# Dense attentions with four score banks, three single key banks, one-bank exponentials and a weighted sum in two halves

## The chip, the cores and the metric

The kernel runs on one core of a Trainium2 chip. The metric is the device time of one execution in microseconds (us); lower is better. A core has a matrix engine (TensorE, PE in the profile, with its weight loads as PEld), VectorE (DVE), ScalarE (ACT), GpSimd (POOL) and a queue engine that issues DMAs (SP). They share the PSUM memory: eight banks of 128 partitions by 512 fp32 values, into which TensorE writes and from which VectorE and ScalarE read.

## The reference, cut to what matters

The program is a stack of twelve sublayers on an activation of 4 sequences by 512 tokens by 128 channels. Only two are touched by the change, the dense attentions with 16 heads of 8 channels each: `mqa` (one shared key and value head, causal) and `rope` (full, not causal).

```python
# mqa                                              # rope
latent = x @ Wc_down                               q, k, v = proj(Wq, bq), proj(Wk, bk), proj(Wv, bv)
q = (latent @ Wq_up).reshape(B, T, 16, 8)          q = _apply_rope(q, cos, sin) * scale
k, v = split(latent @ Wkv_up)                      k = _apply_rope(k, cos, sin)
att = einsum('bthd,bsd->bhts', q, k) * scale       attn = einsum('bhsd,bhtd->bhst', q, k)
att = where(tril, att, -inf)
att = softmax(att, axis=-1)                        attn = softmax(attn, axis=-1)
y = einsum('bhts,bsd->bthd', att, v)               out = einsum('bhst,bhtd->bhsd', attn, v)
x = x + y @ Wc_proj                                x = x + out @ Wo + bo
```

Each stands between feed-forward sublayers (mixture of experts, channel mixing); after them come a gated layer, a forget-gated attention, a deep six-layer block and others, none of which changes.

## The kernel before, in words

All programs are written out by hand, one instruction order for each engine, with counting semaphores between them (`wait_ge`, `then_inc`). The channels of 16 heads are held "wide": a head takes 32 partitions, so that four heads fill the 128 partitions. Four such sets of heads in four sequences make 16 blocks; a block has four tiles of 128 tokens. That gives 64 **groups** for an attention, and the loop over them in `dense_attend_pe` (L571) has 72 **slots**: slot i does three things for three different groups.

- *Scores* of group i (`dense_scores_pe`, L516, matmul L524): four matmuls, head j = 0 to 3 in its own 32 rows of the array, queries of the tile against the keys. VectorE then takes the largest score of every query (`dense_max_dve`, L721: L732 in `rope`, the fused L729 with the causal mask in `mqa`) and so frees the bank.
- *Keys* of group i-6 (`dense_keys_pe`, L536, matmul L550): the same products turned round, keys of a tile on the partitions and the queries along the free dimension, in head order 2, 3, 0, 1. ScalarE takes the exponential into SBUF (`dense_exp_act`, L648, L654).
- The *weighted sum* or *mix* of group i-8 (`dense_mix_pe`, L554, matmul L567): four matmuls, one for each head, in four column groups of the array, all into bank 7; they use all 128 rows. After the fourth tile ScalarE copies the bank away (`dense_y_act`, L657, L659), and the next block's first mix waits for that.

In every fourth slot there is also a *turn* (`dense_max_pe`, L527, L532): four 128x128 matmuls that turn the largest values of a block, which VectorE then adds to the queries (`dense_lay_max_dve`, L734, L737). A turn takes a bank of the same ring as the scores.

In `mqa` the widths follow the causal mask: in the slots i%4 = 0, 1, 2, 3 the scores are 128, 256, 384, 512 wide, the keys 384, 512, 128, 256, and the mix 128, 256, 384, 512; GpSimd zeroes the later keys after the exponentials (`dense_pool`, L781). In `rope` everything is 512 wide.

The PSUM banks before: 0 to 2 are the ring of scores and turns (use v waits until use v-3 is freed), 3 to 6 are two pairs for the keys (pair m waits until the exponential of pair m-2 is done), 7 holds the mix. TensorE executes its queue in order, so whatever stands behind a waiting matmul waits too. The order of a slot before is: score 0, keys of heads 2 and 3, score 1; mix; turn; score 2, keys of heads 0 and 1, score 3.

The probabilities go to one of three buffers (`probs_of`), so an exponential of group g waits for the mix of group g-3.

Of the kernel before, what the change touches and what calls it, by code (L numbers as in the profile page):

```python
# [16 lines left out]
ACT = mybir.ActivationFunctionType  # L17
AX = mybir.AxisListType

P = 128  # L20
NB, T = 4, 512
TILES = T // P
# [23 lines left out]
def program(nc, d, out, sublayers):  # L46
    with ExitStack() as ctx:
# [6 lines left out]
        def bank(i):  # L54
            return psum[:, i * 512:(i + 1) * 512]
# [275 lines left out]
        def moe_dve(dve, u, n, k, b):  # L331
# [32 lines left out]
            for t in range(TILES):  # L364
# [5 lines left out]
                if t >= 2:  # L370
# [18 lines left out]
        dense_counts = {"mqa": da._make([NB, NB, 0, 0, 0, 0, 0, NB, NB, 5 * NB, 5 * NB, 1, 64 * NB, 68 * NB, 4 * NB, 32 * NB,  # L389
                                         32 * NB, 16 * NB, 16 * NB, 4 * NB, NB, NB, NB, NB, NB]),  # L390
                        "rope": da._make([0, 0, NB, NB, 2 * NB, 2 * NB, 6 * NB, 4 * NB, 4 * NB, 8 * NB, 8 * NB, 1, 64 * NB, 68 * NB,
                                          4 * NB, 32 * NB, 32 * NB, 0, 16 * NB, 4 * NB, NB, NB, NB, NB, NB])}
# [23 lines left out]
        SCORE_BANKS = 3  # L416
# [119 lines left out]
        def dense_keys_pe(pe, causal, group, half, N):  # L536

            b, s, kt = group // GROUPS, group // TILES % SETS, key_tile(causal, group)
            q0 = kt * P if causal else 0
            kk = keys_of(causal, b, s)  # L540
            m = 2 * group + half
            if group % TILES == 0 and half == 0:
                pe.wait_ge(da.banks_free, N.banks_free + bank_use[group + TILES, "turn"] + 1)
            if m >= 2:
                pe.wait_ge(da.probs_ready, N.probs_ready + m - 1)
            apart(pe)
            for at in range(2):
                j = KEY_ORDER[2 * half + at]
                r32, to = slice(32 * j, 32 * j + 32), bank(3 + 2 * (m % 2) + at)
                last = nc.tensor.matmul(to[:, q0:T], kk[r32, kt * P:(kt + 1) * P], da_Q[r32, b * SETS + s, q0:T],  # L550
                                        start=True, stop=True)
            last.then_inc(da.keys_ready, 1)

        def dense_mix_pe(pe, causal, group, N):  # L554
            b, s, kt = group // GROUPS, group // TILES % SETS, key_tile(causal, group)
            q0 = kt * P if causal else 0
            first, last_ = group % TILES == 0, group % TILES == TILES - 1
            if causal:
                pe.wait_ge(da.later_zeroed, N.later_zeroed + group + 1)
            pe.wait_ge(da.probs_ready, N.probs_ready + 2 * group + 2)  # L560
            if first and group >= TILES:
                pe.wait_ge(da.y_kept, N.y_kept + group // TILES)
            apart(pe)
            for at in range(SETS):
                j = KEY_ORDER[at]
                c0 = 0 if causal else s * P + 32 * j
                last = nc.tensor.matmul(bank(7)[32 * j:32 * j + 32, q0:T], da_V[:, b * TILES + kt, c0:c0 + 32],  # L567
                                        probs_of(group)[:, at, q0:T], start=first, stop=last_, skip_group_check=True)
            last.then_inc(da.pv_done, 1)

        def dense_attend_pe(pe, causal, N):  # L571
            made = 5 * NB if causal else 8 * NB
            pe.wait_ge(da.wide_kept, N.wide_kept + made)
            pe.wait_ge(da.v_kept, N.v_kept + (NB if causal else NB * TILES))
            for i in range(SLOTS):
                for half in range(2):
                    if half == 1:
                        if i >= MIX_LAG:
                            dense_mix_pe(pe, causal, i - MIX_LAG, N)
                        if turn_of(i) is not None:  # L580
                            dense_max_pe(pe, i, N)
                    if i < GROUPS * NB:
                        dense_scores_pe(pe, causal, i, 2 * half, N)
                    if 0 <= i - LAG < GROUPS * NB:
                        dense_keys_pe(pe, causal, i - LAG, half, N)
                    if i < GROUPS * NB:
                        dense_scores_pe(pe, causal, i, 2 * half + 1, N)

# [59 lines left out]
        def dense_exp_act(act, causal, group, half, N):  # L648
            q0 = key_tile(causal, group) * P if causal else 0
            m = 2 * group + half  # L650
            if half == 0 and group >= 3:
                act.wait_ge(da.pv_done, N.pv_done + group - 2)
            act.wait_ge(da.keys_ready, N.keys_ready + m + 1)
            nc.scalar.activation(probs_of(group)[:, 2 * half:2 * half + 2, q0:T], banks(3 + 2 * (m % 2), 2)[:, :, q0:T],  # L654
                                 ACT.Exp).then_inc(da.probs_ready, 1)
# [5 lines left out]
        def dense_act(act, n, causal, N):  # L661
            dense_prepare_act(act, n, causal, N)
            for group in range(GROUPS * NB + MIX_LAG - LAG):
                mixed = group - (MIX_LAG - LAG)
                if group < GROUPS * NB:
                    dense_exp_act(act, causal, group, 0, N)
                if mixed >= 0 and mixed % TILES == TILES - 1:
                    dense_y_act(act, mixed // TILES, N)
                if group < GROUPS * NB:
                    dense_exp_act(act, causal, group, 1, N)  # L670
# [101 lines left out]
        def dense_pool(pool, u, n, causal, N):  # L772
# [3 lines left out]
            if causal:  # L776
                for group in range(GROUPS * NB):
                    q0 = key_tile(causal, group) * P
                    block = probs_of(group)[:, :, q0:q0 + P]
                    pool.wait_ge(da.probs_ready, N.probs_ready + 2 * group + 2)  # L780
# [1028 lines left out]
```

## Time and profile before

| | before |
|---|---|
| median of 3 runs | 5142.44 us |
| lowest and highest run | 5136.1 and 5149.91 us |
| span of the profiled execution | 5148.7 us |
| busy in the span: PE, DVE, ACT, POOL | 4508.2, 3456.9, 2317.0, 3075.1 us |
| loop of `mqa` (first score to the end of the last mix) | 212.95 to 443.73 us |
| loop of `rope` | about 762 to 1053.00 us |

The profile is of one execution; its span is from the first to the last instruction and lies 6.3 us above the median of the runs. No time around the span is recorded for it. A busy PE is not PE at its peak: matmuls of different rows overlap, and their ends are modelled. One fp32 matmul leaves two records. Where the text says that a matmul takes so long, it is the distance between the starts of two things that can't overlap.

### The profile page before, as it was taken

The numbers are of one execution on the slowest core, as the hardware profiler recorded it, in microseconds if no ns is written. First come the engines' busy times: TensorE is split into PE (matmuls) and PEld (weight loads), VectorE is DVE, ScalarE is ACT, GpSimd is POOL, SyncE is SP. The second block draws the span as 40 slices with busy tenths as digits, with TensorE's granted clock in tenths as the row PEclk, the third lists the DMA queues.
The fourth block names the chain that finished last, engine by engine and source line by source line (L and its number), as shares of the span: only waits on it lengthen the run. The fifth ranks groups of instructions, "written<-read, shape, count | busy, mean of one in ns | idle before, by whom it ended". The sixth has DMA issues, their size and how long they took to land.

```text
span 5148.7 us, 147111 instructions
## 1 busy us (share of the span) xinstructions
PE 4508.2 (88%) x66028; PEld 2555.2 (50%) x66028; DVE 3456.9 (67%) x4153; ACT 2317.0 (45%) x2523; POOL 3075.1 (60%) x1713
## 2 busy tenths in 40 slices
PE   6898689977468999999999999568999999999998
PEld 3444333333135555555555555235555555555554
DVE  4365536632437778778777776447877787888885
ACT  1242134433134555555555555234555555555553
POOL 0010000000019889888889997049988899998984
PEclk7699679976569999999999999669999999999999
DMA  2000000000001112111111111101111111112111
GB/s 71 1 1 1 0 0 1 1 0 0 0 22 32 30 29 55 29 51 32 52 29 53 31 29 33 44 9 29 33 51 30 35 49 30 54 29 55 30 32 29
DMA packets 78094, 144.43 MB, mean 28 GB/s; under 512 B 18728, under 2 KB 24944, under 8 KB 75824
## 3 DMA queue, kind: packets, MB, share of 16 engines
q1 hardware_dynamic: 77488, 135.23, 10.1%
q8 instruction: 517, 8.47, 0.7%
q14 instruction: 89, 0.73, 0.0%
HBM read 39.75 MB, written 1.05 MB: 8 GB/s over the span
## 4 chain that ended last, share of the span: by engine, by line
PE 47%; issue 23%; POOL 21%; DVE 7%; ACT 1%; DMA 0%; SPq 0%; DVEq 0%; POOLq 0%
POOL arena L1446 8%; PE psum L1033 8%; POOL arena L1439 6%; POOL arena L1452 5%; PE psum L1050 4%; PE psum L1064 4%; PE psum L1102 4%; PE psum L1083 4%; PE psum L1002 3%; PE psum L1148 3%; PE psum L1097 2%; PE psum L1142 2%; PE psum L524 2%; POOL rstd L1457 2%; PE psum L1016 2%
## 5 line engine op out<-in xcount | busy, mean ns | idle before, releaser
L1446 POOL TENSOR_TENSOR arena<-arena,minus_half 128x16 f32<-128x16 f32 x384 | 1131.9, 2948 | 32.0
L1439 POOL TENSOR_TENSOR arena<-arena 128x1024 f32<-128x1024 f32 x384 | 909.8, 2369 | 13.5 <-DVE arena L1324 13.5
L1452 POOL TENSOR_TENSOR arena<-arena 128x1024 f32<-128x1024 f32 x384 | 733.7, 1911 | 42.6
L1320 DVE TENSOR_TENSOR arena<-psum,arena 128x1024 f32<-128x1024 f32 x384 | 468.1, 1219 | 404.1 <-ACT arena L1202 404.1
L1462 POOL MEMSET arena<- 128x33 f32 x4 | 0.4, 128 | 995.3 <-DVE std L1686 995.3
L1208 ACT ACTIVATE arena<-psum 128x1024 f32<-128x1024 f32 x384 | 392.2, 1021 | 298.8 <-PE psum L1050 298.4
L1202 ACT ACTIVATE arena<-psum 128x1024 f32<-128x1024 f32 x384 | 392.3, 1022 | 246.5 <-PE psum L1033 243.4
L1324 DVE TENSOR_TENSOR arena<-psum,arena 128x1024 f32<-128x1024 f32 x384 | 466.8, 1215 | 54.1 <-PE psum L1050 54.1
L1050 PEld LDWEIGHTS psum<-w_ident,arena 128*128 128x128 f32 x3072 | 355.3, 141 | 281.9 <-issue 148.5
L1331 DVE TENSOR_REDUCE arena<-arena 128x16 f32<-128x1024 f32 x384 | 464.8, 1211 | 2.8
L1235 ACT ACTIVATE arena<-psum 128x1024 f32<-128x1024 f32 x192 | 196.7, 1024 | 580.7 <-PE psum L1064 580.7
L1050 PE MATMUL psum<-w_ident,arena 128*128 128x128 f32 x3072 | 407.0, 276 | 48.9 <-POOL arena L1452 48.3
L1083 PE MATMUL psum<-arena 64*64 64x32 f32 x24576 | 408.8, 220 | 33.7 <-issue 33.6
L1033 PE MATMUL psum<-deep_wqkv,arena 128*128 128x512 f32 x768 | 388.8, 630 | 36.3 <-DVE arena L1324 28.4
L1083 PEld LDWEIGHTS psum<-arena 64*64 64x64 f32 x24576 | 383.3, 135 | 71.3 <-issue 71.3
L1033 PE MATMUL psum<-arena 128*128 128x512 f32 x768 | 372.8, 607 | 0.0
L1002 PE MATMUL psum<-arena 64*32 64x64 f32 x24576 | 296.4, 224 | 65.8 <-issue 65.2
L524 PE MATMUL psum<-arena 32*128 32x512 f32 (+3 forms) x1024 | 330.2, 593 | 11.9 <-DVE arena L729 9.0
L1002 PEld LDWEIGHTS psum<-arena 64*32 64x32 f32 x24576 | 281.9, 105 | 86.7 <-issue 76.4
L1308 DVE TENSOR_TENSOR arena<-arena 128x1024 f32<-128x1024 f32 x192 | 301.9, 1572 | 5.9
L1219 ACT ACTIVATE arena<-psum 128x1024 f32<-128x1024 f32 x192 | 195.8, 1020 | 242.0 <-PE psum L1016 235.8
L1444 POOL TENSOR_SCALAR arena<-arena 128x16 f32<-128x16 f32 x384 | 153.6, 400 | 245.5 <-DVE arena L1331 245.3
(260 smaller groups left out, 7703.9 us busy)
## 6 DMA issues: line engine op xcount, KB each, us to landing
arena<-arena SPq DMA_DIRECT2D x672, 128.0 KB, 2.3
deep_wqkv<-in_deep_wqkv SPq DMA_DIRECT2D x6, 1536.0 KB, 7.1
arena<-in_deep_wqkv SPq DMA_DIRECT2D x6, 1536.0 KB, 7.2
arena<-arena SPq DMA_DIRECT2D x96, 64.0 KB, 2.5
deep_wo<-in_deep_wo SPq DMA_DIRECT2D x6, 512.0 KB, 7.5
arena<-in_deep_wo SPq DMA_DIRECT2D x6, 512.0 KB, 7.4
deep_w<-in_deep_w SPq DMA_DIRECT2D x6, 341.0 KB, 7.6
arena<-in_deep_w SPq DMA_DIRECT2D x6, 341.0 KB, 7.5
```

The lines of the kernel that those rows point to most:

```text
L524: nc.tensor.matmul(bank(v % SCORE_BANKS)[:, 0:keys], da_Q[r32, b * SETS + s, x_ * P:(x_ + 1) * P], keys_of(causal, b, s)[r32, 0:keys], sta ...
L1002: last = nc.tensor.matmul(bank(r)[32 * jj:32 * jj + 32, pair * 64:pair * 64 + 64], qT[r64, pair, wi * WIN:(wi + 1) * WIN], kT[r64, pair, w ...
L1033: last = nc.tensor.matmul(bank(2 + cc), xs[unit_ % 2][:, WIN + t * P:WIN + (t + 1) * P], wqkv[:, half * INNER + cc * 512:half * INNER + (c ...
L1050: last = nc.tensor.matmul(turns[:, m * P:(m + 1) * P], roped[:, h:h + 2, :], w.ident[:, :], start=True, stop=True, is_transpose=True)
L1083: last = nc.tensor.matmul(bank(odd)[64 * side:64 * side + 64, to:to + WIN], V[64 * r:64 * r + 64, WPT * t + jj, (pair + odd) * 64:(pair + ...
L1202: nc.scalar.activation(qk_sq[:, HALVES[half], :], qk_half, ACT.Square).then_inc(de.deep_qk_squared, 1)
L1320: nc.vector.tensor_tensor(turned[:, hs, :].rearrange("p h (a e) -> p h a e", a=2), swapped, sin, ALU.mult).then_inc(de.deep_rope_parts, 1)
L1324: nc.vector.tensor_tensor(roped[:, hs, :], qk_half, under(tabs[:, 2 * half, t, :], shape), ALU.mult).then_inc(de.deep_rope_parts, 1)
L1331: nc.vector.tensor_reduce(h_sum[a % 2][:, hs], qk_sq[:, hs, :], AX.X, ALU.add).then_inc(de.deep_sq_summed, 1)
L1439: nc.gpsimd.tensor_tensor(roped[:, hs, :], roped[:, hs, :], turned[:, hs, :], ALU.add).then_inc(de.deep_summed, 1)
L1446: nc.gpsimd.tensor_tensor(h_inv[a % 2][:, hs], h_inv[a % 2][:, hs], minus_half[:, :], ALU.pow).then_inc(de.deep_inv_ready, 1)
L1452: nc.gpsimd.tensor_tensor(roped[:, hs, :], roped[:, hs, :], over(h_inv[a % 2][:, hs], [P, LHEADS, LD]), ALU.mult).then_inc(de.deep_roped, 1)
```

## The change

The ring of scores gets four banks, 0 to 3. The keys get three single banks, 4 to 6, in a ring of matmuls (bank 4 + m % 3): each of the four key matmuls of a group waits for the exponential of the third one before it, and each exponential covers one bank of 512 and not two. Bank 7 stays. The mix is cut in two halves of its columns, except in the first group of a block, whose mix stays whole because it starts the accumulation. The new order of a slot is: score 0, keys of heads 2 and 3, score 1; first half of the mix; turn; score 2, keys of heads 0 and 1, score 3; second half of the mix. The counts of `keys_ready` and `probs_ready` double. ScalarE now does all four exponentials of a group and then the copy of bank 7, which before stood between the two exponentials.

```diff
-        SCORE_BANKS = 3
+        SCORE_BANKS, KEY_BANKS = 4, 3
...
+        def key_bank(m):
+            return bank(SCORE_BANKS + m % KEY_BANKS)
+
-        def dense_keys_pe(pe, causal, group, half, N):
+        def dense_keys_pe(pe, causal, group, at, N):
...
-            m = 2 * group + half
-            if group % TILES == 0 and half == 0:
+            m = SETS * group + at
+            if group % TILES == 0 and at == 0:
                 pe.wait_ge(da.banks_free, N.banks_free + bank_use[group + TILES, "turn"] + 1)
-            if m >= 2:
-                pe.wait_ge(da.probs_ready, N.probs_ready + m - 1)
+            if m >= KEY_BANKS:
+                pe.wait_ge(da.probs_ready, N.probs_ready + m - KEY_BANKS + 1)
             apart(pe)
-            for at in range(2):
-                j = KEY_ORDER[2 * half + at]
-                r32, to = slice(32 * j, 32 * j + 32), bank(3 + 2 * (m % 2) + at)
-                last = nc.tensor.matmul(to[:, q0:T], kk[r32, kt * P:(kt + 1) * P], da_Q[r32, b * SETS + s, q0:T],
-                                        start=True, stop=True)
-            last.then_inc(da.keys_ready, 1)
-
-        def dense_mix_pe(pe, causal, group, N):
+            j = KEY_ORDER[at]
+            r32 = slice(32 * j, 32 * j + 32)
+            nc.tensor.matmul(key_bank(m)[:, q0:T], kk[r32, kt * P:(kt + 1) * P], da_Q[r32, b * SETS + s, q0:T],
+                             start=True, stop=True).then_inc(da.keys_ready, 1)
+
+        def dense_mix_pe(pe, causal, group, part, N):
...
+            middle = T if first else (q0 + T) // 2
+            lo, hi = (middle, T) if part else (q0, middle)
+            if lo == hi:
+                return
...
-                last = nc.tensor.matmul(bank(7)[32 * j:32 * j + 32, q0:T], da_V[:, b * TILES + kt, c0:c0 + 32],
-                                        probs_of(group)[:, at, q0:T], start=first, stop=last_, skip_group_check=True)
-            last.then_inc(da.pv_done, 1)
+                last = nc.tensor.matmul(bank(7)[32 * j:32 * j + 32, lo:hi], da_V[:, b * TILES + kt, c0:c0 + 32],
+                                        probs_of(group)[:, at, lo:hi], start=first, stop=last_, skip_group_check=True)
+            if hi == T:
+                last.then_inc(da.pv_done, 1)
...
             for i in range(SLOTS):
                 for half in range(2):
-                    if half == 1:
-                        if i >= MIX_LAG:
-                            dense_mix_pe(pe, causal, i - MIX_LAG, N)
-                        if turn_of(i) is not None:
-                            dense_max_pe(pe, i, N)
                     if i < GROUPS * NB:
                         dense_scores_pe(pe, causal, i, 2 * half, N)
                     if 0 <= i - LAG < GROUPS * NB:
-                        dense_keys_pe(pe, causal, i - LAG, half, N)
+                        dense_keys_pe(pe, causal, i - LAG, 2 * half, N)
+                        dense_keys_pe(pe, causal, i - LAG, 2 * half + 1, N)
                     if i < GROUPS * NB:
                         dense_scores_pe(pe, causal, i, 2 * half + 1, N)
+                    if i >= MIX_LAG:
+                        dense_mix_pe(pe, causal, i - MIX_LAG, half, N)
+                    if half == 0 and turn_of(i) is not None:
+                        dense_max_pe(pe, i, N)
...
-            nc.scalar.activation(probs_of(group)[:, 2 * half:2 * half + 2, q0:T], banks(3 + 2 * (m % 2), 2)[:, :, q0:T],
-                                 ACT.Exp).then_inc(da.probs_ready, 1)
+            nc.scalar.activation(probs_of(group)[:, at, q0:T], key_bank(m)[:, q0:T], ACT.Exp).then_inc(da.probs_ready, 1)
...
                 if group < GROUPS * NB:
-                    dense_exp_act(act, causal, group, 0, N)
+                    for at in range(SETS):
+                        dense_exp_act(act, causal, group, at, N)
                 if mixed >= 0 and mixed % TILES == TILES - 1:
                     dense_y_act(act, mixed // TILES, N)
-                if group < GROUPS * NB:
-                    dense_exp_act(act, causal, group, 1, N)
```

## Rows read from the trace of the kernel before

**Rows 1.** The head of the page.
```profile
span 5148.7 us, 147111 instructions
```

**Rows 2.** Busy time by stretch: loop of `mqa`, start and loop of `rope`.
```profile
core 0: us, PE busy (x) PEld busy (x) DVE busy (x) ACT busy (x) POOL busy (x), PEclk, DMA share, GB/s
240.00:432.00 192.00, 182.39 (x1487) 87.70 (x1488) 124.22 (x462) 87.82 (x129) 36.12 (x57) 0.99 0.01 1
762.00:788.00 26.00, 24.97 (x60) 13.22 (x64) 15.63 (x25) 1.52 (x2) 0.00 (x0) 0.54 0.00 1
788.00:1037.00 249.00, 249.00 (x1512) 86.30 (x1509) 159.63 (x248) 124.01 (x131) 0.00 (x0) 0.99 0.00 1
```

**Rows 3.** Timeline of PE over two slots of `rope`, the first with a turn.
```profile
812.86 1.06 PE L567 MATMUL psum<-arena 128*32 128x512 f32 x8
813.85 1.16 PE L532 MATMUL psum<-w_ident,arena 128*128 128x128 f32 x8
814.94 0.69 PE L524 MATMUL psum<-arena 32*128 32x512 f32 x1
...
816.03 0.70 PE L550 MATMUL psum<-arena 32*128 32x512 f32 x2
...
817.96 1.06 PE L567 MATMUL psum<-z,arena 128*32 128x512 f32 x8
818.95 0.69 PE L524 MATMUL psum<-arena 32*128 32x512 f32 x1
818.96 0.70 PE L550 MATMUL psum<-arena 32*128 32x512 f32 x2
...
819.91 0.59 PE L550 MATMUL psum<-arena 32*128 32x512 f32 x1
...
820.95 1.09 PE L524 MATMUL psum<-arena 32*128 32x512 f32 x2
821.97 1.07 PE L567 MATMUL psum<-arena 128*32 128x512 f32 x8
```

**Rows 4.** Timeline of VectorE and ScalarE in the same slots.
```profile
815.05 0.69 DVE L737 TENSOR_TENSOR arena<-psum,arena 128x512 f32<-128x512 f32 x1 [1.39 <-PE psum L532]
...
820.11 1.89 DVE L732 TENSOR_REDUCE arena<-psum 128x1 f32<-128x512 f32 x3 [1.35 <-PE psum L524]
820.17 1.02 ACT L654 ACTIVATE arena<-psum 128x1024 f32<-128x1024 f32 x1 [1.89 <-PE psum L550]
```

**Rows 5.** Timeline of the end of `rope`: last turn, then slots without scores.
```profile
1035.60 1.16 PE L532 MATMUL psum<-w_ident,arena 128*128 128x128 f32 x8
1036.69 1.14 PE L550 MATMUL psum<-arena 32*128 32x512 f32 x8
...
1037.76 1.07 PE L567 MATMUL psum<-arena 128*32 128x512 f32 x8
1037.87 1.02 ACT L654 ACTIVATE arena<-psum 128x1024 f32<-128x1024 f32 x1 [2.03 <-PE psum L550]
...
1039.04 1.57 PE L550 MATMUL psum<-arena 32*128 32x512 f32 x6 [0.21 <-ACT arena L654]
...
1053.00 1.13 PE L596 MATMUL psum<-arena 128*128 128x512 f32 x2
```

**Rows 6.** Groups of ScalarE by shape in the loop of `mqa`.
```profile
L654 ACT ACTIVATE arena<-psum 128x512 f32<-128x512 f32 x18 | 10.7, 597 | 5.4 <-PE psum L550 4.3
...
L654 ACT ACTIVATE arena<-psum 128x256 f32<-128x256 f32 x18 | 6.9, 381 | 13.4 <-PE psum L550 13.4
```

**Rows 7.** Timeline of VectorE at the start of `rope`, scores alone.
```profile
772.33 1.89 DVE L732 TENSOR_REDUCE arena<-psum 128x1 f32<-128x512 f32 x3 [1.03 <-PE psum L524]
```

**Rows 8.** Timeline of PE in `mqa`: two turns, and a mix of 256.
```profile
308.95 1.16 PE L532 MATMUL psum<-w_ident,arena 128*128 128x128 f32 x8
...
335.57 1.16 PE L532 MATMUL psum<-w_ident,arena 128*128 128x128 f32 x8
...
338.81 0.64 PE L567 MATMUL psum<-z,arena 128*32 128x256 f32 x8
339.38 0.48 PE L524 MATMUL psum<-arena 32*128 32x256 f32 x1
```

More of the change, by code:

```diff
@@ L388, in program @@
                   "inv_ready ysum_ready y_ready out_ready")
-        dense_counts = {"mqa": da._make([NB, NB, 0, 0, 0, 0, 0, NB, NB, 5 * NB, 5 * NB, 1, 64 * NB, 68 * NB, 4 * NB, 32 * NB,
-                                         32 * NB, 16 * NB, 16 * NB, 4 * NB, NB, NB, NB, NB, NB]),
+        dense_counts = {"mqa": da._make([NB, NB, 0, 0, 0, 0, 0, NB, NB, 5 * NB, 5 * NB, 1, 64 * NB, 68 * NB, 4 * NB, 64 * NB,
+                                         64 * NB, 16 * NB, 16 * NB, 4 * NB, NB, NB, NB, NB, NB]),
                         "rope": da._make([0, 0, NB, NB, 2 * NB, 2 * NB, 6 * NB, 4 * NB, 4 * NB, 8 * NB, 8 * NB, 1, 64 * NB, 68 * NB,
-                                          4 * NB, 32 * NB, 32 * NB, 0, 16 * NB, 4 * NB, NB, NB, NB, NB, NB])}
+                                          4 * NB, 64 * NB, 64 * NB, 0, 16 * NB, 4 * NB, NB, NB, NB, NB, NB])}
         SETS = 4
@@ L557, in dense_mix_pe @@
             first, last_ = group % TILES == 0, group % TILES == TILES - 1
[L558 to L562, printed above, removed]
+            middle = T if first else (q0 + T) // 2
+            lo, hi = (middle, T) if part else (q0, middle)
+            if lo == hi:
+                return
+            if part == 0:
+                if causal:
+                    pe.wait_ge(da.later_zeroed, N.later_zeroed + group + 1)
+                pe.wait_ge(da.probs_ready, N.probs_ready + SETS * (group + 1))
+                if first and group >= TILES:
+                    pe.wait_ge(da.y_kept, N.y_kept + group // TILES)
             apart(pe)
@@ L646, in dense_prepare_act, with dense_exp_act @@
                     nc.scalar.activation(to, bank(4 + at % 2), ACT.Identity, bias=w.da_one[:, :]).then_inc(da.wide_kept, 1)
-        def dense_exp_act(act, causal, group, half, N):
+        def dense_exp_act(act, causal, group, at, N):
             q0 = key_tile(causal, group) * P if causal else 0
-            m = 2 * group + half
-            if half == 0 and group >= 3:
+            m = SETS * group + at
+            if at == 0 and group >= 3:
                 act.wait_ge(da.pv_done, N.pv_done + group - 2)
             act.wait_ge(da.keys_ready, N.keys_ready + m + 1)
-            nc.scalar.activation(probs_of(group)[:, 2 * half:2 * half + 2, q0:T], banks(3 + 2 * (m % 2), 2)[:, :, q0:T],
-                                 ACT.Exp).then_inc(da.probs_ready, 1)
+            nc.scalar.activation(probs_of(group)[:, at, q0:T], key_bank(m)[:, q0:T], ACT.Exp).then_inc(da.probs_ready, 1)
         def dense_y_act(act, q, N):
@@ L779, in dense_pool @@
                     block = probs_of(group)[:, :, q0:q0 + P]
-                    pool.wait_ge(da.probs_ready, N.probs_ready + 2 * group + 2)
+                    pool.wait_ge(da.probs_ready, N.probs_ready + SETS * (group + 1))
                     nc.gpsimd.affine_select(block, block, [[0, SETS], [1, P]], ALU.is_ge, 0.0, base=0,
```

## The prediction

> **What bounds the kernel now.** I read the page first: one execution spans 5148.7 us [rows 1]. The windows then show how little of that the change touches: the two attention loops hold about 232 and 290 us, and in each TensorE is busy nearly throughout while VectorE has 64% and ScalarE 46 to 50% of the stretch [rows 2]. The granted clock is 0.99 in both loops, the 2.4 GHz level, and 0.54, the 1.2 GHz level for most of it, in the first slots of `rope`, when scores stand alone.
>
> Busy does not mean full, so I went to the timeline of PE for one slot of `rope` [rows 3]. From mix to mix is 821.97 - 817.96 = 4.01 us. The mix takes 0.99 (817.96 to 818.95). Then come score 2, two keys and score 3 together, and, since each row group is free again after 0.96 (818.96 to 819.91), the next slot's score 0 and keys. All of that would be drained near 820.8. Score 1 however starts alone at 820.95 and holds the mix back to 821.97, 1.02 us. What it waited for is in the view of VectorE [rows 4]: its reduce begins at 820.11, 1.16 after the score, lasts 0.68 (1.89 for three, partly overlapped), and 0.15 later TensorE goes on. That is the ring of three banks: one matmul in four runs with three of four row groups empty. In the slot with a turn the distance is 817.96 - 812.86 = 5.10: the turn takes 1.09, and score 0 at about 816.0 waits for VectorE to have emptied the turn's bank (815.05 + 0.69 + 0.15). Turn to turn, four slots, is (1035.60 - 813.85) / 13 = 17.06 us [rows 3, 5].
>
> **Prices.** All for a 512-wide matmul at full clock:
> - phase of four matmuls started together, then something that needs all rows: 1.07 (1036.69 to 1037.76) [rows 5]; one started late adds 1.02 from its own start [rows 3]
> - mix, whole 0.99 [rows 3]; 256 wide 0.57 (338.81 to 339.38) [rows 8]. So 1.64 ns a column and 0.15 fixed: the cut costs 2 x 0.57 - 0.99 = 0.15 a slot.
> - exponential of one bank: 0.597, from the 18 exponentials of 2 x 256 columns [rows 6]. The lower bound, were only the columns to count, is half of the 1.02 of two banks [rows 5], 0.51; the upper bound is 1.02 itself. I take 0.60, since the row has this very number of columns.
> - key matmul to the start of its exponential: 1.21 (818.96 to 820.17) [rows 3, 4], 1.18 (1036.69 to 1037.87) [rows 5]; I take 1.19. End of an exponential to the next matmul: 1039.04 - 1038.89 = 0.15 [rows 5], I take 0.13 to 0.15.
>
> The last three give the new wait. Key m+3 cannot start before key m + 1.19 + 0.60 + 0.13 = **L = 1.92 us**.
>
> At this step a page bears on the sum. The Trainium skill, "ScalarE: Activation LUTs", rules for kernel authors, budgets about 0.3 us for each ACTIVATE and 0.83 ns an element, so splitting pays the fixed part twice and one bank would take 0.73. The 597 ns of rows 6 are below that, and the trace decides; by the page L would be 2.05 and, at the price per 0.1 us worked out below, the kernel would come to about 5125.
>
> **The change in `rope`.** Phases of four matmuls now alternate with half mixes. Let f be the start of a phase's first pair and s that of its second key and the score queued behind it. Two rules: s is at least L after the f of the phase before (key m waits for key m-3), and the next phase starts s + 1.02 + 0.57 later. From f = 0, s = 0: next f = 1.64, s = 1.92 (0.28 lost); next f = 1.92 + 1.60 = 3.52, s = 3.56. A slot is thus about **3.52** and not 4.01. Without the key wait it would be 3.28.
>
> The slot with a turn starts at 0: phase 1.07; whole mix 0.99, to 2.06; turn 1.09, to 3.15; phase B at 3.15. There is no second half of the mix, so the next slot's score 0 and first key follow at 3.15 + 0.97 = 4.12 (the turn's bank is not theirs; score 1 needs it, free at 2.06 + 1.20 + 0.69 + 0.15 = 4.10). The next key has to wait for the key of 3.15: 5.07. End 6.10, half mix 6.67, phase 7.74, half mix 8.31, where the turn slot's successor ends. Two slots of 3.52 follow: **15.35** for four slots, 1.71 less than 17.06. Times 14 periods (slots 8 to 63): **-23.9 us**.
>
> Nothing else is late there. VectorE needs 16 x 0.68 + 0.69 = 11.6 of 15.35, ScalarE 17 x 0.60 = 10.2. The four exponentials of a group are now ahead of the copy of bank 7. The copy can start 0.13 after the half mix ends, is held by the fourth exponential to about 0.33, and ends near 0.93; TensorE wants it for the next whole mix at 1.07, with 1.06 available: no stall, but no slack either (worth 0.1 us a period at most). The next exponential needs ScalarE at 1.19. The buffers of the probabilities wait for a mix of the slot before, already past. GpSimd does nothing in `rope`; SP has no DMA in either loop that the change moves.
>
> Start: VectorE's three reduces come every 1.89 + 1.03 = 2.92 us [rows 7], a ring of three at its latency. With four banks the same 2.92 carries four (reduces 4 x 0.63 = 2.5 still fit): 0.97 a slot, five to six slots: **-5**, and -1 for the two slots before the mixes begin. End: slots 64 to 71 have keys and mixes but no scores. There the old order is nearly free of waits, 1053.00 - 1036.69 = 16.3 us [rows 5]. The same two rules give 10.56 for the first three slots' end, 12.20, 14.50 behind the last whole mix and 21.9 at the end: **+5.6**. `rope` in all: -24.3.
>
> **The change in `mqa`.** Turn to turn is (335.57 - 308.95) / 2 = 13.31 [rows 8]. The same rules with widths: phase 0.22 + W/600 for the widest W of it, mix 0.15 + W/600 (fits 0.57 and 0.99), L = 0.63 + W/400 for keys W wide (1.91 at 512, 1.59 at 384, 1.27 at 256), where the exponentials' 597 and 381 ns set the slope [rows 6]. From phase B of the turn slot at 0: next slot 0.76, its second key at 1.59, B at 2.98; the slot of 384 scores 4.41, its second key held to 4.89 by a 512-wide one, B 6.17; the slot of 512 scores 7.49, B 9.13; turn slot 10.77, mix 11.63, turn 11.99, B again at **13.08**. That is 0.23 less a period, 14 times: **-3.2 us**. It gains little because four banks help only where the scores are wide, while the cut costs 0.15 in three slots of four and the keys wait twice a period. GpSimd's zeroing (a mix comes two slots after its exponentials) is as far from the path as before. Start and end go as in `rope`, with narrower tiles: about -4 and +3.5, taken as zero together.
>
> **Sum.** -24.3 - 3.2 = **-27.5 us**: the profiled 5148.7 becomes 5121, and the median, which lies 6.3 below the profiled span, 5142.4 becomes **5115**. All later sublayers shift as they are. A measurement of this kernel can tell about 0.3%, 15.4 us, from no change; the three runs of before span 0.27%.
>
> **What L is worth.** Every 0.1 us of L costs three steps a period in `rope` (4.2 us), two in `mqa` (2.8) and some ten in the ends (1): 8 us. So the gain is gone at L = 2.27 and the kernel 0.3% slower at about 2.46.
>
> **Rivals.**
> 1. *The new key wait does not bind*, because pairs overlap better than my two rules (say exponentials begin at the first key's end, or the score behind a held key slips past). For it: 0.28 us is little. Against it: TensorE takes its queue in order and rows 5 show 0.21 us idle for just such an exponential. Slots of 3.28 and no hold behind the turn (1.0 us): 13.9 a period, -44 in `rope` and no loss at its end: about 5090.
> 2. *The key wait takes most of the gain* (within 0.3%). L = 2.1 to 2.3, through a slower handover with twice as many semaphores or a single exponential nearer the upper bound: 5127 to 5145. Against it: all parts of L are read, and none twice.
> 3. *Slower: the chain of the three key banks.* The exponential of one bank costs as much as two (1.02, the upper bound): L = 2.34, with ScalarE at 17 x 0.93 a period just above TensorE, so 15.8 to 16.6 a period, `mqa` worse than before; from L = 2.46 on it is over 0.3% slower, near 5158. Rows 6 speak against it.
> 4. *Slower: the clock.* The loops now hold short idle pieces in every phase, and in the first slots of `rope`, where TensorE waits in every ring turn, the granted clock was 0.54 [rows 2]. At the 1.2 GHz level about 12.9 us of each period would double, so two or three such periods of 28 undo the gain; half of `rope` would cost 90 us, 5205. Against it: the loop before had such waits in each slot at 0.99. The Trainium skill, "TensorE: Matmul & The Clock Gate", section on PSUM-queue depth-cycling, describes a kernel whose clock oscillates because it idles briefly between groups of matmuls while cycling through banks; the trace of before, which cycles through three banks, does not show it.
>
> **Chances and range.** My forecast, 15 to 40 us less: 0.62. Rival 1, more than that: 0.10. Rival 2, within 0.3%: 0.20. Rivals 3 and 4: 0.05 and 0.03. So faster 0.72, same 0.20, slower 0.08. The range: rival 1 near its foot (5095) up to rival 2 at L = 2.2 (5137). Without rivals it would be 5105 to 5125.
>
> **What will show it.** In `rope`: turn to turn near 15.35 with slots of 3.5; reduces of scores without a wait of TensorE for L732; exponentials 512 wide at 0.60, 1.2 behind their key; TensorE waiting on L654's successor where now it waits for VectorE, above all in the slot after a turn, about 1 us. `mqa` near 13.1. The stretch from the last turn to the sums near 22 us. Wrong would be: exponentials far above 0.6, half mixes far from 0.57, a clock below 0.99 in the loops, or a stall of the whole mix on the copy of bank 7.

## The result, and the profile after

The kernel after takes 5168.33 us (median of 7 runs, 5158.81 to 5196.45), the one before 5142.44 on the same chip (7 runs, 5132.21 to 5150.27): a ratio of 1.0057, interval 1.0036 to 1.0078. It is slower, by 26 us and by more than the 0.3% that a measurement can tell, where I forecast 27 us less. The forecast range was 5095 to 5137.

The head of the page after (the column of instructions is the last):

```profile
span 5166.6 us, 149255 instructions
```

I cut both executions at the same marks (first score, turns at L532, first sum) to see where the 17.9 us of span came from.

| part | before | after | change | predicted |
|---|---|---|---|---|
| `rope`, first score to third turn | 51.47 | 44.46 | -7.0 | -6 |
| `rope`, 13 periods | 17.06 each | 16.24 each | -10.7 | -1.71 each, 14 periods |
| `rope`, last turn to sums | 17.39 | 35.44 | +18.0 | +5.6 |
| `mqa`, first score to third turn | 42.77 | 36.00 | -6.8 | -4 |
| `mqa`, 13 periods | 13.30 each | 13.61 each | +4.0 | -3.2 |
| `mqa`, last turn to sums | 15.10 | 26.13 | +11.0 | +3.5 |
| both attentions | 521.39 | 530.04 | +8.6 | -27.5 |
| first deep block (L1002 before, L1008 after, first to last start) | 1659.8 | 1680.6 | +20.8 | 0 |

The rest is -11.5 us: 4.1 ahead of the first attention, 2.9 from there to the deep block, 4.5 behind it. I didn't follow it. The stretch ahead of `mqa` has the same code in all thirteen traces and takes 206.1 to 220.7 us in them, so differences of this size are no effect of the change. Part of the gain at the start of `mqa` is the clock: it stood at 0.50 for the first 32.4 us of that loop before, for 21.0 after, and in e3 below, with the code of the kernel after in that loop, for 49.5.

**The steady slot.** Timeline of the kernel after, one slot of `rope` (start, duration, engine, line; rows that follow closely are merged, so 0.96 at 913.00 is two keys, the second from 913.29):

```profile
911.36 0.70 PE L552 MATMUL psum<-arena 32*128 32x512 f32 x2
...
912.42 0.64 PE L574 MATMUL psum<-z,arena 128*32 128x256 f32 x8
912.55 1.08 ACT L662 ACTIVATE arena<-psum 128x512 f32<-128x512 f32 x2 [1.22 <-PE psum L552]
912.99 0.69 PE L524 MATMUL psum<-arena 32*128 32x512 f32 x1
913.00 0.96 PE L552 MATMUL psum<-arena 32*128 32x512 f32 x2
913.44 0.67 PE L524 MATMUL psum<-arena 32*128 32x512 f32 x2
...
914.47 0.64 PE L574 MATMUL psum<-arena 128*32 128x256 f32 x8
915.03 0.69 PE L524 MATMUL psum<-arena 32*128 32x512 f32 x1
915.14 1.01 PE L524 MATMUL psum<-arena 32*128 32x512 f32 x2
916.16 0.64 PE L574 MATMUL psum<-arena 128*32 128x256 f32 x8
```

Key at 911.36, its exponential at 912.55 (1.19), 0.597 long, 0.14 more to the held key at 913.29: L = 1.93, where I had 1.92. The half mix is 0.57 (912.42 to 912.99), as read. But the score queued behind the held key starts at 913.44 and not with it; the mix comes 1.02 after that score. The next phase, too, loses 0.1 (its second score at 915.14 where its keys are at 915.04, mix 1.02 later). The slot is 916.16 - 912.42 = 3.74 where my rules give 3.52. In the whole loop VectorE and ScalarE stay below TensorE, and the clock is full:

```profile
788.00:1017.00 229.00, 229.00 (x1801) 89.42 (x1796) 155.84 (x241) 129.59 (x240) 0.00 (x0) 1.00 0.00 1
```

ScalarE's group by shape in that loop gives 595 ns for the exponential of one bank [rows 6], and shows that ScalarE now waits for keys:

```profile
L662 ACT ACTIVATE arena<-psum 128x512 f32<-128x512 f32 x146 | 79.8, 595 | 64.3 <-PE psum L552 64.3
```

**The end of `rope`.** Timeline of the kernel after, the answer to [rows 5]:

```profile
1020.17 1.16 PE L532 MATMUL psum<-w_ident,arena 128*128 128x128 f32 x8
...
1023.15 1.09 PE L552 MATMUL psum<-arena 32*128 32x512 f32 x2 [0.77 <-ACT arena L662]
...
1026.37 1.08 PE L574 MATMUL psum<-arena 128*32 128x256 f32 x8
1027.38 2.08 PE L552 MATMUL psum<-arena 32*128 32x512 f32 x4
1029.39 1.08 PE L574 MATMUL psum<-arena 128*32 128x256 f32 x8
...
1055.60 4.69 PE L604 MATMUL psum<-arena 128*128 128x512 f32 x10
```

A pair of keys takes 2.0 us from 1027.38 on and a half mix 1.0, double what both took in the loop. The windows of the two ends, after (the number behind the five engines' pairs is the granted clock):

```profile
421.00:448.00 27.00, 26.38 (x169) 10.10 (x165) 0.99 (x3) 10.91 (x26) 4.10 (x7) 0.63 0.01 1
...
1025.00:1055.00 30.00, 29.23 (x128) 7.27 (x130) 0.00 (x0) 10.33 (x19) 0.00 (x0) 0.50 0.00 1
```

With the scores gone the granted clock is 0.50, the 1.2 GHz level, for all of this stretch of `rope` (30.7 us without a break), and for 20.5 us at `mqa`'s end. Before it was 1.00 in both ends (1035 to 1053, 428 to 444). PE is "busy" for 29.23 of 30.00 us there: this figure doesn't show the loss; the clock column does. The section on PSUM-queue depth-cycling that the prediction draws on (the Trainium skill, "TensorE: Matmul & The Clock Gate") describes short idle times between groups of matmuls and a clock that goes back and forth. This trace does not bear it out: the records hold hardly any idle time, only row groups without work, and the clock fell once and stayed low.

**The deep block.** Its code is the same in both kernels. Groups of the page, before and then after; the last column is PE's idle time ahead of them and what ended it:

```profile
L1083 PE MATMUL psum<-arena 64*64 64x32 f32 x24576 | 408.8, 220 | 33.7 <-issue 33.6
...
L1002 PE MATMUL psum<-arena 64*32 64x64 f32 x24576 | 296.4, 224 | 65.8 <-issue 65.2
```

```profile
L1089 PE MATMUL psum<-arena 64*64 64x32 f32 x24576 | 415.4, 220 | 53.4 <-issue 53.2
...
L1008 PE MATMUL psum<-arena 64*32 64x64 f32 x24576 | 300.2, 224 | 79.3 <-issue 79.0
```

"Issue" is idle time in which PE waited for nothing that the profile shows; it grew by 33.4 us over the two lines. One such pause in the timeline of weight loads, after:

```profile
1952.08 0.99 PEld L1008 LDWEIGHTS psum<-arena 64*32 64x32 f32 x73
1955.32 0.62 PEld L1008 LDWEIGHTS psum<-arena 64*32 64x32 f32 x55 [2.25 <-issue]
```

Counting TensorE's records in order, pauses of 0.6 us and more between weight loads inside runs of these two lines lie a multiple of 256 instructions apart: before mostly one in 1280, after mostly two in 1280 (1024 and 256 apart). In the first deep block that is 51 pauses (57.6 us) before, 69 (81.8 us) after.

The DMA rows of the two pages name a queue for instructions, before and then after (packets, MB, share):

```profile
q8 instruction: 517, 8.47, 0.7%
...
q8 instruction: 524, 8.59, 0.7%
```

Each of these packets is 16,384 bytes. In the first deep block 237 of them land before and 236 after, where TensorE passes 238 and 237 times another 256 of its records: one packet for 256 instructions. In all thirteen traces every pause of the kind above stands at the same remainder of the count by 256 (to within one record), and ends 1.04 to 1.63 us (median about 1.4) after the end of such a packet; the one shown ends at 1955.32, and its packet ran from 1952.82 to 1953.86.

TensorE's program ahead of this block grew by 1888 records (11274 to 13162: 768 matmuls, as many weight loads, 352 waits), which is 7 x 256 + 96: every later instruction has another place modulo 256. So I had two theories for the 20.8 us, place of the code or the changed attentions, and two for the rest: waits in the loop's queue, and the clock at the ends.

### The profile page after: what moved, and what is told of

Its sections match the earlier page's. It is cut to its first block, busy times and chain, and to the rows that moved or that the text cites. A ratio compares the mean times of both kernels' runs of the same rounds, so it can differ in the third digit from the quotient of the medians.

```text
span 5166.6 us, 149255 instructions
## 1 busy us (share of the span) xinstructions
PE 4522.4 (88%) x66796; PEld 2569.4 (50%) x66796; DVE 3454.1 (67%) x4153; ACT 2337.9 (45%) x2779; POOL 3065.3 (59%) x1713
## 4 chain that ended last, share of the span: by engine, by line
PE 46%; issue 24%; POOL 22%; DVE 7%; ACT 1%; DMA 0%; SPq 0%; DVEq 0%; POOLq 0%
POOL arena L1452 8%; PE psum L1039 7%; POOL arena L1445 6%; POOL arena L1458 5%; PE psum L1070 4%; PE psum L1056 4%; PE psum L1108 4%; PE psum L1008 3%; PE psum L1089 3%; PE psum L1154 3%; PE psum L1103 2%; PE psum L524 2%; PE psum L1148 2%; POOL rstd L1463 2%; PE psum L1022 1%
## 5 line engine op out<-in xcount | busy, mean ns | idle before, releaser
L1241 ACT ACTIVATE arena<-psum 128x1024 f32<-128x1024 f32 x192 | 196.5, 1024 | 597.9 <-PE psum L1070 597.9
L1056 PE MATMUL psum<-w_ident,arena 128*128 128x128 f32 x3072 | 407.5, 276 | 38.5 <-POOL arena L1458 36.1
L1039 PE MATMUL psum<-deep_wqkv,arena 128*128 128x512 f32 x768 | 389.5, 631 | 36.1 <-DVE arena L1330 28.2
L1008 PE MATMUL psum<-arena 64*32 64x64 f32 x24576 | 300.2, 224 | 79.3 <-issue 79.0
L1008 PEld LDWEIGHTS psum<-arena 64*32 64x32 f32 x24576 | 284.0, 105 | 102.8 <-issue 92.5
L524 PE MATMUL psum<-arena 32*128 32x512 f32 (+3 forms) x1024 | 310.7, 589 | 2.4 <-ACT arena L654 1.7
L1450 POOL TENSOR_SCALAR arena<-arena 128x16 f32<-128x16 f32 x384 | 143.1, 373 | 272.7 <-DVE arena L1337 272.5
L552 PE MATMUL psum<-arena 32*128 32x512 f32 (+3 forms) x1024 | 299.0, 585 | 5.3 <-ACT arena L662 3.4
```

Of the source, the lines that this page charges most:

```text
L524: nc.tensor.matmul(bank(v % SCORE_BANKS)[:, 0:keys], da_Q[r32, b * SETS + s, x_ * P:(x_ + 1) * P], keys_of(causal, b, s)[r32, 0:keys], sta ...
L1008: last = nc.tensor.matmul(bank(r)[32 * jj:32 * jj + 32, pair * 64:pair * 64 + 64], qT[r64, pair, wi * WIN:(wi + 1) * WIN], kT[r64, pair, w ...
L1039: last = nc.tensor.matmul(bank(2 + cc), xs[unit_ % 2][:, WIN + t * P:WIN + (t + 1) * P], wqkv[:, half * INNER + cc * 512:half * INNER + (c ...
L1056: last = nc.tensor.matmul(turns[:, m * P:(m + 1) * P], roped[:, h:h + 2, :], w.ident[:, :], start=True, stop=True, is_transpose=True)
```

## The experiments

Ratios of the experiments are to the kernel before as measured beside them (its medians: 5150.51 for e1 to e4, 5149.18 for e5 to e8, 5145.46 for e9 to e11), so compare ratios and not medians across these groups. "Place" is that of the first deep matmul in TensorE's records, modulo 256.

| run | place | ratio (interval) | median | `rope` | `mqa` | first deep block |
|---|---|---|---|---|---|---|
| before, profiled | 10 | | 5142.44 | 290.61 | 230.78 | 1659.8 |
| after, profiled | 106 | 1.0057 (1.0036 to 1.0078) | 5168.33 | 290.98 | 239.06 | 1680.6 |
| e1_before_pad96 | 106 | 1.0046 (1.0030 to 1.0061) | 5172.55 | 289.76 | 230.21 | 1680.0 |
| e2_after_pad160 | 10 | 1.0018 (1.0007 to 1.0029) | 5158.91 | 289.47 | 238.49 | 1660.6 |
| e3_after_filled | 106 | 1.0028 (1.0013 to 1.0043) | 5166.31 | 278.02 | 245.49 | 1678.9 |
| e4_after_ahead | 106 | 0.9987 (0.9973 to 1.0001) | 5141.53 | 269.36 | 221.42 | 1674.0 |
| e5_ahead_pad160 | 10 | 0.9947 (0.9928 to 0.9966) | 5125.51 | 271.12 | 226.40 | 1660.3 |
| e6_ahead_tailwhole | 10 | 0.9937 (0.9919 to 0.9955) | 5117.26 | 271.14 | 222.92 | 1657.1 |
| e7_after_whole | 10 | one run | 5204.49 | 311.73 | 258.86 | 1661.2 |
| e8_after_3_4 | 106 | one run | 5168.41 | 275.00 | 237.71 | 1677.8 |
| e9_before_pad256 | 10 | 0.9999 (0.9988 to 1.0010) | 5144.68 | 289.65 | 230.79 | 1660.8 |
| e10_3_4_pad160 | 10 | 0.9970 (0.9957 to 0.9984) | 5130.72 | 274.99 | 229.14 | 1660.5 |
| e11_ahead_filled | 10 | 0.9938 (0.9917 to 0.9959) | 5112.89 | 269.68 | 221.21 | 1662.3 |

### The place of the code: e1, e2, e9

The kernel before with 96 instructions more on TensorE, and later with 256; the kernel after with 160 (16 each time), so that 96 + 160 is 256:

```
 # in forget_out_pe, which runs between the attentions and the deep block
+                for _ in range(min(10, 96 - 10 * i)):
+                    apart(pe)
```

> The kernel before with 96 extra semaphore instructions in TensorE's program, spread over the ten steps of the forget-gated attention where TensorE mostly waits. The changed kernel's TensorE program is 1888 instructions longer ahead of the deep block, and 1888 is 96 more than a multiple of 256; the unexplained pauses of about 1 us inside runs of matmuls stand at distances of 256 instructions in both traces. Theory A (the place of the deep block in TensorE's program decides how many such pauses fall on its critical path): the first deep block lengthens by about 13 us as in the changed kernel, the whole to 5150 to 5165 us, 0.2 to 0.4% over the kernel before, and pauses appear twice in 1280 instructions (1024 and 256 apart) and not once. Theory B (the later start, or chance, made the deep block slow): no difference, ratio 1.000 within 0.15%. The attention loops must read as before, 230.8 and 290.6 us.

> The changed kernel with 160 such instructions in the same place, which makes the difference of length to the kernel before 2048, a multiple of 256. Theory A: the deep block goes back to its time before, 13 to 16 us less, the whole to 5150 to 5155 us, a ratio near 1.002 and not 1.0057. Theory B: stays at 5165 to 5170. The attentions must read as in the changed kernel, 239.1 and 291.0 us, since nothing in them differs.

> The kernel before with 256 extra semaphore instructions where the first run had 96. Theory (only the remainder of the place by 256 counts): the first deep block stays at 1660 us with about 50 pauses, the whole within 0.15% of the kernel before. Rival (more instructions in that place cost time by themselves, in proportion): more than twice the first run's loss, a ratio of 1.01 or so.

96 instructions that do nothing make the kernel before 0.46% slower, its first deep block 1680.0 long, with 71 pauses (85.5 us) in my count; 256 of them leave it at 0.9999 and 1660.8, with 53 pauses. The kernel after, put back in place, goes from 1680.6 to 1660.6. The rows of the pages, e1 first, then e2:

```profile
L1085 PE MATMUL psum<-arena 64*64 64x32 f32 x24576 | 414.5, 220 | 55.9 <-issue 55.7
...
L1004 PE MATMUL psum<-arena 64*32 64x64 f32 x24576 | 299.7, 224 | 87.5 <-issue 87.3
```

```profile
L1091 PE MATMUL psum<-arena 64*64 64x32 f32 x24576 | 407.5, 220 | 31.7 <-issue 31.5
...
L1010 PE MATMUL psum<-arena 64*32 64x64 f32 x24576 | 297.1, 224 | 74.1 <-issue 73.5
```

The issue idle of both lines follows the place and not the attentions: 98.8 us before, 105.0 in e2, and 132.2 after, 143.0 in e1. Not the number of added instructions but their number modulo 256 decides, as e9 shows. That is some 20 of the 26 us. Two remainders were tried, 10 and 106; others may cost more or less.

### The clock at the ends: e3

The kernel after with matmuls into free score banks on row groups 0 to 2, once a phase, in the slots that have keys and no scores. Nothing reads them.

```
+        def dense_fill_pe(i, half):
+            for j in ((0, 1) if half == 0 else (2,)):
+                r32 = slice(32 * j, 32 * j + 32)
+                nc.tensor.matmul(bank(j)[:, 0:T], da_Q[r32, 0, 0:P], da_Q[r32, 0, 0:T], start=True, stop=True)
...
+                    elif (i, half) >= (GROUPS * NB, 1) and i - LAG < GROUPS * NB:
+                        dense_fill_pe(i, half)
```

> The changed kernel with extra matmuls, whose results nobody reads, in the row groups that stand empty in the slots without scores (slots 64 to 69 of each attention): two 512-wide ones beside each first pair of keys, one beside each second pair. Its padding keeps the distance of the deep block's code a multiple of 256 from the changed kernel's. Theory clock (the granted clock falls in these slots because half the array's work is gone and each phase waits for an exponential): it stays at 1.0, the stretch from the last turn to the sums goes from 35.4 to 22 to 24 us in rope and from 26.1 to 17 to 20 in mqa, 18 to 21 us together, and the whole to about 5150. Theory waits (the tails are long by the waits for exponentials alone and the clock only follows): the tails stay above 30 and 24 us, or the clock falls all the same. The periods of the loops stay 16.24 and 13.61.

Windows of e3 over the ends of `mqa` and `rope`:

```profile
437.00:458.00 21.00, 20.08 (x192) 8.26 (x190) 0.69 (x1) 10.42 (x26) 3.82 (x6) 1.00 0.01 2
...
1031.00:1053.00 22.00, 22.00 (x184) 8.21 (x188) 0.69 (x1) 12.43 (x23) 0.00 (x0) 1.00 0.00 1
```

The clock stays at 1.00, `rope`'s end takes 22.57 instead of 35.44, `mqa`'s 20.83 instead of 26.13. More work in it made the stretch 13 us shorter. From the last turn on my two rules give 17.39 + 5.6 = 23.0 for `rope`; 22.57, with the added matmuls in it, is 0.4 below, so they hold at full clock. `mqa` is just above the 17 to 20 expected. The whole came to 5166, not to the 5150 expected: the ratio is 1.0028 where after has 1.0057, but the two intervals overlap, and the profiled execution had a low clock at the start of `mqa` (46.44 to the third turn, where after has 36.00). So the total of this run doesn't say what the filling is worth.

### The order in the phase: e4, e5, e11

The second score of a phase goes ahead of its second key, the one that is held:

```
                     if 0 <= i - LAG < GROUPS * NB:
                         dense_keys_pe(pe, causal, i - LAG, 2 * half, N)
-                        dense_keys_pe(pe, causal, i - LAG, 2 * half + 1, N)
                     if i < GROUPS * NB:
                         dense_scores_pe(pe, causal, i, 2 * half + 1, N)
+                    if 0 <= i - LAG < GROUPS * NB:
+                        dense_keys_pe(pe, causal, i - LAG, 2 * half + 1, N)
```

> The changed kernel with the second score of each phase put ahead of its second key, so that no score stands behind a key that waits for an exponential. My prediction took such a score to start together with the held key; the trace shows it 0.15 us later (913.29 and 913.44). Theory queue (each instruction behind a held one pays another wake-up of 0.15, and the next phase starts that much later): non-turn slots of rope go from 3.74 to about 3.55, the period from 16.24 to 15.6 to 15.8, mqa from 13.61 to about 13.3. Theory chain (only the distance key to key m+3 of 1.93 us sets the period): no change, 16.24 and 13.61. The tails stay as they are, 35 and 26 us.

> Both cures together: the score ahead of the held key as in the fourth run, and the 160 extra instructions of the second run, so that the deep block's code stands as in the kernel before. Theory (the two effects are separate and add): attentions as in the fourth run, 221 and 269 us, first deep block 1660 us and not 1674 to 1681, the whole about 15 to 20 us below the fourth run's 5141.5, 5122 to 5127 us, ratio 0.995 to 0.9965 to the kernel before. Rival (the fourth run was fast by chance, its deep block included): no gain over it, ratio 0.998 to 1.000.

> The fifth run (score ahead of the held key, deep block's code in place) with the idle row groups of the last slots filled as in the third. Theory clock: no stretch of lower clock from the last turn to the sums, which take 22.4 us in rope and 20 to 21 in mqa against 24.0 and 25.9, so attentions near 220 and 269 and the whole 5 us below the fifth, 5115 to 5120 us, ratio 0.993 to 0.995. Theory waits: no change against the fifth.

Timeline of e4, one phase of `rope`:

```profile
915.47 0.69 PE L524 MATMUL psum<-arena 32*128 32x512 f32 x1
915.48 0.69 PE L552 MATMUL psum<-arena 32*128 32x512 f32 x1
915.48 0.69 PE L524 MATMUL psum<-arena 32*128 32x512 f32 x1
915.77 0.66 PE L552 MATMUL psum<-arena 32*128 32x512 f32 x1
916.79 0.64 PE L574 MATMUL psum<-arena 128*32 128x256 f32 x8
```

The held key is 0.29 late (915.77 against 915.48) and nothing stands behind it; the mix comes 1.02 after its own start, not after a score that is 0.15 later still. The period falls from 16.24 to 15.65, that of `mqa` from 13.61 to 12.76, further than the 13.3 expected. (In `mqa` a score can be wider than the key beside it and now starts without waiting for it; that this makes the difference is argued, not tested.) The ends shortened too (`rope` 22.35, no low clock there; `mqa` 20.77, 6.8 us of low clock), against my expectation: the slots without scores have the same instructions in the same order in e4 as in the kernel after. At place 10 (e5) it is 0.9947; the low clock of `mqa` was longer again there (20.5 us, from 411.3 on). e11 adds the filling: both ends at full clock (22.57 and 20.83), and 0.9938. Its ends are no shorter than e4's, which has no filling: where the clock stays up by itself, the filling gains nothing.

### The cut of the mix: e6, e7

e6 is e5 with the mix uncut in the slots behind the last scores, e7 the kernel after with no cut at all:

```
-            middle = T if first else (q0 + T) // 2
+            middle = T if first or group + MIX_LAG > GROUPS * NB else (q0 + T) // 2   # e6
+            middle = T                                                                # e7
```

> As the fifth, but in the slots after the last score the mix is not cut: one whole mix in the first half of the slot, so that the second pair of keys and the next slot's first pair meet without a mix between them. Padded so that the deep block's code stands as in the kernel before. Theory (a cut mix between pairs of keys makes each pair pay the full 1.93 us and gives the clock a reason to fall): the stretch from the last turn to the sums goes from 22.4 to 17 to 19 us in rope and from 20.8 to 15 to 17 in mqa, together 8 us less than in the fifth, the whole near 5115 to 5119. Rival (with three single banks the fourth key of such a chain waits as long anyway): tails within 1 us of 22.4.

> The changed kernel with the cut of the mix undone: the mix is whole after the first phase of a slot, nothing after the second, everything else as changed. Read in the loops alone. If the cut is what lets the ring of three key banks keep up (it puts 0.57 us between each two phases): period of rope above 16.24, up to 17, since the second phase runs straight into the next slot's first and the next key waits a full 1.93 us. If the cut only costs its 0.15 us a slot: 15.8 to 16.0.

e6: `rope`'s end is 24.06 with the clock at 1.00, where e4 has 22.35 at the same clock and e5 24.01 with 3.4 us of low clock in it. So the whole mixes cost 1.7 us there instead of gaining the 3 to 5 expected, and the rival was nearer. In `mqa` (end 22.51) 10.2 us of low clock were left. e7 is far slower. Timeline of one slot of it:

```profile
902.47 0.66 PE L552 MATMUL psum<-arena 32*128 32x512 f32 x1
902.62 0.66 PE L524 MATMUL psum<-arena 32*128 32x512 f32 x1
903.64 1.07 PE L574 MATMUL psum<-arena 128*32 128x512 f32 x8
...
907.75 1.07 PE L574 MATMUL psum<-arena 128*32 128x512 f32 x8
```

Mix to mix is 4.11, more than the 4.01 of before, and the period 17.55, beyond the 17 that I had expected at most (`mqa` 14.48): without the half mix between the groups, the second phase of a slot comes before L has passed. The 0.15 between a held key (902.47) and the score behind it (902.62) shows here too.

### Which banks: e8, e10

The kernel after with three banks for scores and four for keys; e10 is the same with 160 instructions more, at place 10:

```
-        SCORE_BANKS, KEY_BANKS = 4, 3
+        SCORE_BANKS, KEY_BANKS = 3, 4
```

> The changed kernel with the eight banks shared out as 3 for the scores and 4 for the keys. Read in the loops alone. The key wait then reaches back four matmuls and should no longer hold anything (two phases, over 3.2 us); the score wait reaches back three: a score needs the bank of the third one before it, 1.16 + 0.68 + 0.15 = 1.99 us after that one's start. If a held instruction costs the same wherever it stands, rope comes to 16.0 to 16.6, like the changed kernel's 16.24; if the fourth score bank was what freed the loop, it returns to 17 or more; if the key chain was the only limit, it falls to 15.0 to 15.5.

> The eighth run (three score banks, four key banks, one-bank exponentials, cut mix) with 160 extra instructions, which put the deep block's code where it stands in the kernel before. Theory: loops as in the eighth run (15.86 a period in rope, 13.1 in mqa, tails 19.5 and 16), first deep block 1660, attentions 275 and 232 to 238 us depending on when the clock rises, the whole 5125 to 5135 us, ratio 0.996 to 0.998. So three and four banks would be a gain where four and three were a loss. Rival: the clock falls in its tails too, ratio near 1.000.

Without touching the order of the queue, a period of `rope` is 15.86 and most periods of `mqa` are 13.12, and the ends are 19.48 and 16.08 with no low clock: the fourth bank is worth more to the keys than to the scores in this order. Against that stand longer starts (in `rope` 49.4 us to the third turn, where after has 44.46), and the total of e10, 0.9970, lies behind e5's 0.9947 with intervals that overlap.

## Why the prediction was wrong

The prices were right; three steps failed. Against the forecast, the deep block adds 20.8 us. The attentions add 36.1 (8.6 for -27.5): some 20 of these are the periods, 20 the ends, and the starts gave 4 back. The rest of the span took 11.5 off again.

**"All later sublayers shift as they are": wrong, +20.8 us.** The largest term was one I had put at zero. The edit lengthened TensorE's program by 1888 instructions ahead of an unrolled block of thousands of small matmuls, and the block met 69 pauses where it had met 51. e1 makes it out of the kernel before with nothing but idle instructions (+20.2), e9 and e2 take it back. That it is caused by the place modulo 256 is shown. That a pause is a wait for the next 256 instructions is what the traces point to: one packet of the instruction queue for each 256 records, and every pause ends 1.04 to 1.63 us behind the end of one. No run changed the fetching itself, and what fills that time is open. The second deep block is less clear: 1650.6 before, 1657.8 to 1661.3 at place 106 in e1, e3, e4 and e8, but 1651.6 in the kernel after.

**The rule "s + 1.02 + 0.57", with key and queued score at the same s: off by 0.22 a slot.** The score behind a held key starts 0.15 after it, and four slots cost 16.24 and not 15.35: 12 us over `rope`, and in `mqa` (13.61 for 13.08) 7 us, enough to turn a small gain into a loss. L itself, the exponential (0.595 to 0.597) and the half mix were right to 0.02. The 0.73 for one bank that the prediction worked out from the Trainium skill, "ScalarE: Activation LUTs", rules for kernel authors, was the wrong price to take: that rule is for an ACTIVATE whose bias is a pointer operand. The exponentials have no such operand and took 0.595 to 0.597; a 128x512 activation that has one (L646 before) took 0.687. Rival 1 named "the score behind a held key" as something that could slip past; it did the reverse. e4 is the proof by removal: with no score behind the held key the period of `rope` is 15.65. The last 0.3 is a slip of my sum. It let each pair of slots begin with no key held, and put the first phase of the turn slot at 1.07. In e4 that phase takes 1.20 (907.01 to the mix at 908.21), since its second key is held to 907.19. By my estimate the same two rules, carried on through the turn slot, give 15.55 a period, 15.6 with the measured L, and 16.15 to 16.2 with 0.15 more behind each of the four held keys, where the kernel after has 16.24.

**"+5.6" and "+3.5" for the ends, at full clock: +18.0 and +11.0.** Rival 4 named the fall to the 1.2 GHz level, but in the wrong place and for a reason, short idle pieces, that the ends don't show: I priced it in the loops, which stayed at 1.00, and left it out of the slots with keys and half mixes alone, though it was the start of `rope`, scores alone, that showed 0.54 [rows 2]. e3 has no low clock and gives 22.57 (e4, without filling, 22.35), so the clock is 12.9 of `rope`'s 18.0. The remainder is the 5 us that I had. In `mqa` it is at least 5.3 of 11.0: e3's 20.83 has the added matmuls in it, and e4 is as short with 6.8 us of low clock. What makes the clock fall is open. With four score banks and three key banks and no filling it fell, for 3 to 34 us, at four of six ends of `rope` and at all six of `mqa` (after, e2, e4 to e7). With the filling (e3, e11) or with four key banks (e8, e10) it fell at none of eight.

What held: the starts (-7.0 for -6), the wait of TensorE for VectorE gone from the slots, no stall of the whole mix on the copy of bank 7, GpSimd and DMA off the path. Rivals 2 and 3 are out: L was 1.93. With the place kept, the change costs 0.18% (e2); with the order and the ends mended as well it is 0.6% faster than before (e11, 5112.89), near the 5115 that I had forecast for the plain change. That is luck, for it comes by an order of the queue that I had not looked at. e6 and e5 can't be told from e11.

## What to carry to other kernels

Put an instruction that may be held last in its group, and sum a queue with what stands behind the held one, not only the wait itself. A stretch that loses some of its parallel work should be costed at both levels of the clock, the lower one if a sparse stretch of the old trace shows it. If it drops, filling idle row groups with work that nobody reads is worth a try. When an edit changes the length of an unrolled program, compare a block behind it that did not change: here 96 idle instructions cost 0.46%, nearly what the best form of the redesign gains (0.6%), so a change is to be judged at a fixed place modulo 256, by padding both.

## What was not expected of the hardware

- TensorE paused for 0.6 to 3.1 us at distances that are multiples of 256 of its instructions in two unrolled loops of small matmuls, and went on 1.04 to 1.63 us after a packet of 16,384 bytes on the instruction queue had ended; whether once or twice in 1280 depended on the program's length ahead of it modulo 256 (first deep block: 1657.1 to 1662.3 us in the eight executions at place 10, 1674.0 to 1680.6 in the five at place 106).
- A matmul queued behind one that was released by ScalarE started 0.15 us after it, in other row groups (913.29 and 913.44; 902.47 and 902.62 in e7).
- The granted clock went to 0.50 in a stretch whose PE column reads 29.23 of 30.00 us, and stayed at 1.00 when three matmuls for each two phases were added there (e3). In e4 and e5, where the instructions of that stretch are those of the kernel after and only the order ahead of it differs, it was 1.00 in all or most of `rope`'s end. When it fell in `mqa` differed from run to run (6.8 us in e4, 20.5 in e5, the same loop); why is open.
